# Two pairs at a time: scores and mixes merged in the first attention block, steps between engines reassigned and reordered

## The reference

```
xs = roll(x, (-3, -3));  windows of 7 x 7 -> (2048 windows, 49 tokens, 96)
q, k, v = windows @ qkv_w + qkv_b           # 12 heads of 8
attn = (q . k) / clip(|q| |k|, 1e-6) / clip(tau, 0.01) + bias + mask
out  = softmax(attn) @ v @ proj_w + proj_b  # windows and roll undone
x = x + LN(out) * g1 + b1
x = x + LN(gelu(x @ fc1_w + fc1_b) @ fc2_w + fc2_b) * g2 + b2
```

## Time and profile before

| | us |
|---|---|
| median of 3 runs (7351.54 to 7354.21) | 7353.15 |
| the profiled execution | 7355.68 |
| its span, first to last instruction | 7353.9 |
| TensorE busy (span 7353.9) | 7179.3, 98% |
| ScalarE busy | 6373.4, 87% |
| VectorE busy | 5991.6, 81% |
| GpSimd busy | 5233.9, 71% |
| 16 transfer engines, mean busy share | about 11% |

### The profile page before, as it was taken

The page is one execution under the profiler, slowest core; times in us unless marked ns, Lnnn a source line. Parts: engine busy times, 40 slices in busy tenths (PEclk is TensorE's granted clock), DMA queues, the critical chain, the costliest instruction groups (busy, mean ns, idle before and its releaser), DMA issues. The chain is left out here.

```text
span 7353.9 us, 317113 instructions
## 1 busy us (share of the span) xinstructions
PE 7179.3 (98%) x113246; PEld 5509.1 (75%) x113246; DVE 5991.6 (81%) x12718; ACT 6373.4 (87%) x12032; POOL 5233.9 (71%) x5957
## 2 busy tenths in 40 slices
PE   6999999999999999999999996999999999999999
PEld 4777777777777777777777775777777777777777
DVE  5888888888888888888888885777777777777776
ACT  5999999999999999989999986887887887887887
POOL 3777777777777777777777775666666666666665
PEclk9999999999999999999999998999999999999999
DMA  0111111111111111111111101111111111111111
GB/s 21 30 30 30 29 30 30 29 29 31 30 30 29 30 30 30 29 29 30 29 30 29 30 25 24 30 30 29 30 30 29 30 30 29 30 30 29 30 30 26
DMA packets 342624, 214.39 MB, mean 29 GB/s; under 512 B 265624, under 2 KB 341144, under 8 KB 341144
## 3 DMA queue, kind: packets, MB, share of 16 engines
q1 hardware_dynamic: 341146, 194.49, 10.7%
HBM read 78.66 MB, written 77.07 MB: 21 GB/s over the span
## 5 line engine op out<-in xcount | busy, mean ns | idle before, releaser
L881 POOL TENSOR_TENSOR swin_score<-swin_score,swin_top 113x588 f32<-113x588 f32 x1024 | 1203.1, 1175 | 743.6 <-DVE swin_top L753 743.2
L624 ACT ACTIVATE swin_probT<-swin_ps_probs 128x339 f32<-128x339 f32 x2048 | 922.1, 450 | 199.2 <-PE swin_ps_probs L481 178.2
L1553 POOL TENSOR_TENSOR plain_k_heads<-plain_k_hat,plain_head_mask 96x512 f32<-96x512 f32 x392 | 398.9, 1037 | 897.1 <-DVE plain_k_hat L1444 897.1
L481 PE MATMUL swin_ps_probs<-swin_ident,swin_prob 113*128 113x113 f32 x6144 | 991.1, 270 | 7.0 <-ACT swin_probT L624 7.0
L481 PEld LDWEIGHTS swin_ps_probs<-swin_ident,swin_prob 113*128 113x128 f32 x6144 | 667.7, 141 | 355.6 <-issue 321.5
L748 DVE TENSOR_TENSOR swin_score<-swin_ps_scores,swin_bias_tab 113x588 f32<-113x588 f32 x1024 | 777.1, 759 | 174.1 <-PE swin_ps_scores L471 172.9
L753 DVE TENSOR_REDUCE swin_top<-swin_score 113x12 f32<-113x588 f32 x1024 | 769.0, 751 | 0.2
L630 ACT ACTIVATE swin_prob<-swin_score 113x588 f32<-113x588 f32 x1024 | 719.1, 702 | 5.8 <-POOL swin_score L881 2.9
L1431 DVE TENSOR_REDUCE plain_top<-plain_ps_scores 128x6 f32<-128x384 f32 x784 | 432.7, 552 | 263.0 <-PE plain_ps_scores L1206 263.0
L784 DVE SCALAR_TENSOR_TENSOR swin_x<-swin_y,swin_y_rstd,swin_x_res 98x96 f32<-98x96 f32 x1024 | 601.1, 644 | 0.8 <-POOL swin_y_rstd L899 0.7
L495 PEld LDWEIGHTS swin_ps_mixed<-swin_probT,swin_v_heads 128*32 128x32 f32 x24576 | 422.3, 109 | 222.2 <-issue 146.0
(11 more groups left out here) (187 smaller groups left out, 20907.6 us busy)
## 6 DMA issues: line engine op xcount, KB each, us to landing
...
plain_x_in<-between_blocks SPq DMA_DIRECT2D x784, 48.0 KB, 2.2
out_dram<-plain_x SPq DMA_DIRECT2D x784, 48.0 KB, 2.0
...
```

Of the source, the lines that this page charges most:

```text
L481: last = nc.tensor.transpose(psP[:, n * QT:(n + 1) * QT], prob[0:QT, p, 2 * hp:2 * hp + 2, :].rearrange('p h k -> p (h k)'), ident[0:QT, 0 ...
L624: nc.scalar.activation(to, psP[:, 0:3 * QT], ACT.Copy).then_inc(did['probT'], 1)
L881: nc.gpsimd.tensor_tensor(view, view, bcast(top[0:QT, p % 2, :], 2, WIN), ALU.subtract).then_inc(did['shifted'], 1)
```

## The change

- `scores(d, h)` makes the scores of two pairs (2h and 2h + 1) in one step, in two column ranges of the same banks, with one semaphore step. `mix(d, h)` does the mixes of two pairs and then their sums in one step.
- `score` and `top` have four buffers, one to a pair, instead of two.
- `residual`: GpSimd multiplies y by its power in place (`scale_y`, new), and VectorE adds `x_res` in one instruction over all four pairs, in place of four instructions with multiply and add.
- `spread_values` moves from ScalarE to VectorE (two `tensor_copy`).
- The norms lie in dense banks A and B instead of B and C; `project` moves to bank A.
- The four orders are written anew. SyncE's order is unchanged.

Core of the diff (indentation cut; the last waits that only count in halves instead of pairs are left out):

```diff
-score = sb('score', [128, 2, SC])
-top = sb('top', [128, 2, heads])
+score = sb('score', [128, PAIRS, SC])
+top = sb('top', [128, PAIRS, heads])
...
+def earlier_half(g, h):
+return (g, 0) if h else (g - 1, 1)
...
-    def scores(d, p):
+    def scores(d, h):
         if exists(g + d, groups):
             pe.wait_ge(did['q_hat'], upto(g + d))
             pe.wait_ge(did['k_spread'], spread_total(g + d))
-            ug, us = before(g + d, p, 1)
-            pe.wait_ge(did['score_read'], upto(ug, us, PAIRS))
-            for half in range(2):
-                w = 2 * p + half
-                rows = HALF if half == 0 else WIN
-                for band in range(BANDS):
-                    part = slice(32 * band, 32 * band + 32)
-                    last = nc.tensor.matmul(psS[half * HALF:half * HALF + rows, band, 0:BC], q_hat[part, parity(d), w * WIN:w * WIN + rows], k_heads[part, parity(d), :, w * WIN:(w + 1) * WIN], start=True, stop=True)
+            ug, uh = earlier_half(g + d, h)
+            pe.wait_ge(did['score_read'], upto(ug, 2 * uh + 1, PAIRS))
+            for p in (2 * h, 2 * h + 1):
+                for half in range(2):
+                    w = 2 * p + half
+                    rows = HALF if half == 0 else WIN
+                    for band in range(BANDS):
+                        part = slice(32 * band, 32 * band + 32)
+                        last = nc.tensor.matmul(psS[half * HALF:half * HALF + rows, band, p % 2 * BC:(p % 2 + 1) * BC], q_hat[part, parity(d), w * WIN:w * WIN + rows], k_heads[part, parity(d), :, w * WIN:(w + 1) * WIN], start=True, stop=True)
             last.then_inc(did['scored'], 1)
...
-    def mix(d, p):
+    def mix(d, h):
         if exists(g + d, groups):
             pe.wait_ge(did['v_heads'], upto(g + d))
-            pe.wait_ge(did['probT'], upto(g + d, 2 * p + 1, 2 * PAIRS))
-            if p % 2 == 0:
-                mg, ms = before(g + d, p, 2)
-                pe.wait_ge(did['mixedT'], upto(mg, ms // 2, 2))
-            for half in range(2):
-                first = p % 2 * TT + half * WIN
-                for n in range(HB):
-                    for band in range(BANDS):
-                        last = nc.tensor.matmul(psO[32 * band:32 * band + 32, first:first + WIN], v_heads[:, (phase + d) % 4, 2 * p + half, band, n, :], probT[:, p, band * HB + n, half * HALF:half * HALF + WIN], start=n == 0, stop=n == HB - 1)
-            if p % 2 == 1:
-                for n in range(HB):
-                    for band in range(BANDS):
-                        last = nc.tensor.matmul(psO[32 * band:32 * band + 32, SUMS:SUMS + 2 * TT], sum_heads[:, n, :], all_windows(probT[:, p - 1:p + 1, band * HB + n, 0:WIN]), start=n == 0, stop=n == HB - 1)
+            pe.wait_ge(did['probT'], upto(g + d, 2 * (2 * h + 1) + 1, 2 * PAIRS))
+            mg, mh = earlier_half(g + d, h)
+            pe.wait_ge(did['mixedT'], upto(mg, mh, 2))
+            for p in (2 * h, 2 * h + 1):
+                for half in range(2):
+                    first = p % 2 * TT + half * WIN
+                    for n in range(HB):
+                        for band in range(BANDS):
+                            nc.tensor.matmul(psO[32 * band:32 * band + 32, first:first + WIN], v_heads[:, (phase + d) % 4, 2 * p + half, band, n, :], probT[:, p, band * HB + n, half * HALF:half * HALF + WIN], start=n == 0, stop=n == HB - 1)
+            for n in range(HB):
+                for band in range(BANDS):
+                    last = nc.tensor.matmul(psO[32 * band:32 * band + 32, SUMS:SUMS + 2 * TT], sum_heads[:, n, :], all_windows(probT[:, 2 * h:2 * h + 2, band * HB + n, 0:WIN]), start=n == 0, stop=n == HB - 1)
             last.then_inc(did['mixed_made'], 1)
...
-    free(('q_read', 1), ('hid', -4, 1, CHUNKS), ('x1T_low', -4), ('xT', 1))
-    turn_in(2, A)
-    free(('v_heads', 1), ('hid', -4, 2, CHUNKS), ('fc2_read', -5), ('sq_norm', 0))
-    query_norms(1, B)
-    turn_probs(-1, 1, 0)
     scores(0, 0)
     mix(-1, 0)
-    turn_probs(-1, 1, 1)
-    free(('sq_norm', 1), ('k_read', 1), ('hid', -4, 0, CHUNKS), ('proj_read', -3))
-    project(-2, C)
-    free(('xT', 2), ('q_read', 1), ('hid', -4, 1, CHUNKS), ('x1T_low', -4))
-    turn_x1(-3, A)
     turn_probs(-1, 2, 0)
-    free(('sq_norm', 1), ('v_heads', 1), ('hid', -4, 2, CHUNKS), ('fc2_read', -5))
-    output(-4, B)
+    free(('v_heads', 1), ('hid', -4, 0, CHUNKS), ('proj_read', -3), ('sq_norm', 0))
+    query_norms(1, A)
+    free(('k_read', 1), ('hid', -4, 1, CHUNKS), ('x1T_low', -4), ('sq_norm', 0))
+    key_norms(1, B)
+    free(('q_read', 1), ('hid', -4, 2, CHUNKS), ('fc2_read', -5), ('xT', 1))
+    turn_in(2, C)
     turn_probs(-1, 2, 1)
+    free(('sq_norm', 1), ('v_heads', 1), ('hid', -4, 0, CHUNKS), ('proj_read', -3))
+    project(-2, A)
+    free(('sq_norm', 1), ('k_read', 1), ('hid', -4, 1, CHUNKS), ('x1T_low', -4))
+    turn_x1(-3, B)
+    free(('xT', 2), ('q_read', 1), ('hid', -4, 2, CHUNKS), ('fc2_read', -5))
+    output(-4, C)
+    turn_probs(-1, 3, 0)
+    free(('proj_read', -2), ('sq_norm', 1), ('v_heads', 1), ('hid', -4, 0, CHUNKS))
+    hidden(-3, 0, A)
+    turn_probs(-1, 3, 1)
+    free(('x1T_low', -3), ('sq_norm', 1), ('k_read', 1), ('hid', -4, 1, CHUNKS))
+    hidden(-3, 1, B)
+    free(('fc2_read', -4), ('xT', 2), ('q_read', 1), ('hid', -4, 2, CHUNKS))
+    hidden(-3, 2, C)
+    turn_probs(0, 0, 0)
+    scores(0, 1)
     mix(-1, 1)
-    scores(0, 1)
-    turn_probs(-1, 3, 0)
-    free(('proj_read', -2), ('sq_norm', 1), ('k_read', 1), ('hid', -4, 0, CHUNKS))
-    hidden(-3, 0, C)
-    free(('x1T_low', -3), ('xT', 2), ('q_read', 1), ('hid', -4, 1, CHUNKS))
-    hidden(-3, 1, A)
-    free(('fc2_read', -4), ('sq_norm', 1), ('v_heads', 1), ('hid', -4, 2, CHUNKS))
-    hidden(-3, 2, B)
-    scores(0, 2)
-    turn_probs(-1, 3, 1)
-    free(('hid', -3, 0, CHUNKS), ('proj_read', -2), ('sq_norm', 1), ('k_read', 1))
-    keys(2, C)
-    mix(-1, 2)
-    free(('hid', -3, 1, CHUNKS), ('x1T_low', -3), ('xT', 2), ('q_read', 1))
-    queries(2, A)
-    turn_probs(0, 0, 0)
-    mix(-1, 3)
-    free(('hid', -3, 2, CHUNKS), ('fc2_read', -4), ('sq_norm', 1), ('v_heads', 1))
-    values(2, B)
-    scores(0, 3)
+    free(('hid', -3, 0, CHUNKS), ('proj_read', -2), ('sq_norm', 1), ('v_heads', 1))
+    values(2, A)
     turn_probs(0, 0, 1)
-    free(('k_read', 2), ('hid', -3, 0, CHUNKS), ('proj_read', -2), ('sq_norm', 1))
-    key_norms(2, C)
+    free(('hid', -3, 1, CHUNKS), ('x1T_low', -3), ('sq_norm', 1), ('k_read', 1))
+    keys(2, B)
+    turn_probs(0, 1, 0)
+    free(('hid', -3, 2, CHUNKS), ('fc2_read', -4), ('xT', 2), ('q_read', 1))
+    queries(2, C)
+    turn_probs(0, 1, 1)
...
-    def spread_values(d, bank):
-        if exists(g + d, groups):
-            act.wait_ge(did['v_made'], upto(g + d))
-            act.wait_ge(did['mixed_made'], upto(g + d - 4, PAIRS - 1, PAIRS))
-            for odd in range(2):
-                rows = slice(odd * HALF, odd * HALF + WIN)
-                made = psM[rows, bank, 0:WINDOWS * HP * D].rearrange('r (w n d) -> r w n d', n=HB, d=D)
-                last = nc.scalar.activation(own_heads((phase + d) % 4, odd), made, ACT.Copy)
-            last.then_inc(did['v_heads'], 1)
...
-    copy_x(2, A)
-    copy_turned(-1, 1, 0)
+    copy_turned(-1, 1, 1)
+    square_qk(1)
     exponentials(-1, 2)
-    high_x(2, A)
-    copy_turned(-1, 1, 1)
+    log_totals(-1, 0)
+    copy_turned(-1, 2, 0)
+    invert_totals(-1, 0)
+    exponentials(-1, 3)
+    copy_x(2, C)
+    high_x(2, C)
+    exponentials(0, 0)
+    copy_turned(-1, 2, 1)
+    high_x1(-3, B)
+    square_y(-2, A)
     log_norms(1)
-    high_x1(-3, A)
-    square_y(-2, C)
-    copy_turned(-1, 2, 0)
     invert_norms(1)
-    exponentials(-1, 3)
-    copy_turned(-1, 2, 1)
-    exponentials(0, 0)
-    log_totals(-1, 0)
-    invert_totals(-1, 0)
     copy_turned(-1, 3, 0)
+    exponentials(0, 1)
+    copy_turned(-1, 3, 1)
     act.preload_act_table_set(GELU_SET)
-    gelu(-3, 0, C)
-    gelu(-3, 1, A)
-    copy_turned(-1, 3, 1)
-    gelu(-3, 2, B)
+    gelu(-3, 0, A)
+    gelu(-3, 1, B)
+    gelu(-3, 2, C)
+    copy_turned(0, 0, 0)
     act.preload_act_table_set(EXP_SET)
-    exponentials(0, 1)
-    copy_turned(0, 0, 0)
-    square_qk(2)
+    copy_turned(0, 0, 1)
     log_totals(-1, 1)
-    spread_values(2, B)
-    copy_turned(0, 0, 1)
     invert_totals(-1, 1)
+    copy_turned(0, 1, 0)
...
-            dve.wait_ge(did['y_rstd'], upto(g + d))
-            dve.wait_ge(did['proj_read'], upto(g + d))
+            dve.wait_ge(did['y_norm'], upto(g + d))
             dve.wait_ge(did['x_res'], upto(g + d))
             dve.wait_ge(did['x1_turned'], upto(g + d - 1))
             dve.wait_ge(did['x1_res'], upto(g + d - 1))
-            for p in range(PAIRS):
-                last = nc.vector.scalar_tensor_tensor(x1[:, p, :], y[:, p, :], y_rstd[:, p:p + 1], x_res[:, (phase + d) % 4, p, :], ALU.mult, ALU.add)
-            last.then_inc(did['x1'], 1)
```

(69 more changed lines are left out.)

32 lines of the change are left out of this document (15 added, 17 removed).

## The result

The changed kernel takes 7700.3 us (median; 7696.5 to 7703.1), the one before, run beside it, 7352.3. The ratio is 1.047 (95%: 1.046 to 1.049): slower, as predicted, but by 348 us where 7575 stood for 222. The time is beyond the upper end of the range, 7650. The profiled execution's span is 7699.7.

A forecast was written before the change was run, and what follows sets the result against it. TensorE was taken to bound the kernel at 16.78 us a body; after the change the ring, 17.34, plus 0.33 for the load gives 17.67, +0.89 times 256, +228, forecast 7575 us, range 7420 to 7650.

The forecast's parts named there:

- The merge: On TensorE, merged steps and fewer changes of kind (14 to 7) shorten the body by 0.89 us, 16.78 to 15.89.
- (a): TensorE's projection, now in dense bank A, waits for floor_norms: 0.65 us a body, plus 0.07 of weights.
- (b): TensorE's transposes wait in three places for ScalarE's copy from the one bank of turned probabilities: 0.45 us a body.
- TensorE's own length: TensorE's body with its local waits but no wait on the chain through all engines: 17.05 us.
- the ring: Chain of waiting steps through all engines, from one projection to the next, that decides the body: 17.34 us.
- R3: Rival: floor_norms is done before the bank is needed, so the kernel is faster, 7317 down to 7125 us; chance 0.10.
- (c): Step reckoning the chain through all engines, with scale_y, the held residual and values' copies: 17.34 us a body.
- R1: Rival: VectorE's residual add isn't held up; body 17.42 us with the load, +164, 7517 us; chance 0.21.
- the case that I had priced at 0.3: GpSimd's epsilon behind gain_z also holds VectorE's residual add, making the ring some 0.3 us longer.
- (d): SyncE's later load with wrapped rows delays the keys every eighth body: 2.65 us for the ring, 0.33 a body.
- R2: Rival: the load doesn't hold the keys back; +143 or +69, 7496 to 7422 us; chance 0.15.
- R4: Rival: the add held as long as before, or values costing 1.3; ring 17.65 or more, 7655 us and up; chance 0.12.

The follow-up runs named there:

- a2_swap: Changed kernel with ScalarE's exponentials of pair 2 put ahead of its squares (square_qk); 7616.9 us.
- a3_both: Changed kernel with two edits: GpSimd's residual_x one body ahead, and ScalarE's exponentials of pair 2 ahead of its squares; 7434.7 us.
- a4_gain_late: Changed kernel with GpSimd's residual_x one body ahead and its gain_z moved behind the power of z; 7432.6 us.
- d1_one_copy: Changed kernel with residual_x one body ahead and only the first of VectorE's two values' copies made, leaving out part of the computation; 7430.8 us.
- d2: Changed kernel with residual_x one body ahead and VectorE's values' copies shortened, leaving out part of the computation; 7475.7 us.
- a1_load_early: Changed kernel with GpSimd's residual_x one body ahead, behind the power of z, so that SyncE's loads come earlier; 7567.5 us.

## Why the prediction was right in kind and wrong in size

**The merge** and **(a), (b).** TensorE's own length was predicted as 17.05. The four kernels in which the ring is shortened below it (a2_swap, a3_both, a4_gain_late, d1_one_copy) stand at 16.97 to 16.99, by three different edits. The steps are as reckoned: scores 0.82 for 0.83, mixes with sums 1.50 for 1.50, the projection 1.88 after the key norms (2030.24 to 2032.12) for 1.94, `floor_norms` 0.97, transposes 1.05 apart (2023.79 to 2024.84) where one product stands between. What the merge saves on the transposes (0.22) and on the MLP, keys and queries (0.09) was not measured by itself; it is only borne out by the sum. R3 falls on the one distance of 1.88.

**(c), the ring.** Predicted 17.34, found 17.56. From the projection to VectorE's resuming after `residual` it is 2022.37 + 17.56 - 2032.12 = 7.81, predicted 6.46 + 1.30 = 7.76. `scale_y` takes 0.82 for 0.83, `residual` holds VectorE for 1.27 where I had 1.3 (R1 falls; a4_gain_late shows what it would have been). Biases and maxima 2.71 for 2.74. The values 1.14 for 0.92 (2025.08 to 2026.22). From there to the squares 1.50 for 1.43, to the transposes 1.51 for 1.54, to the next projection 2.89 for 2.95. The term that was mis-sized is the values' copies: I had ScalarE's 0.48 each and bounds of 0.8 and 1.3, and took a value near the lower end, without a reason, for an engine of which no such copy was in the trace; VectorE takes 0.55 each. That is 0.22 of the 0.22, 56 us in 256 bodies, and d2 shows that these copies pass into the body undiminished.

How `residual` is held: the Trainium skill (SBUF — State Buffer, Who interferes with whom) says that a VectorE instruction with two SBUF inputs and a GpSimd one that reads SBUF exclude one another for a whole instruction, and that the later one waits. Here the trace agrees as to who waits. `gain_z` started first (2021.03), `residual` 0.07 later, ended 0.42 after it; GpSimd's epsilon, in its turn the later one, took 0.52, where it takes 0.20 elsewhere. `low_x` is the second case: 0.94 beside `residual_x`, 0.56 in a1_load_early, where that step lies elsewhere. My 1.3 rested on a guess ("held until shortly before the end of `gain_z`"); the rows say that the add finishes 0.42 after `gain_z`, a little sooner than its 0.56 would have it if nothing overlapped. That 1.3 came out so close is in part luck. GpSimd's epsilon behind `gain_z` did not hold the add as well, the case that I had priced at 0.3; why the instruction of 1.67 in the earlier trace rows did sit through a second step stays open.

**(d), the wrapped load.** R2 falls: the keys are late by 2.64 (predicted 2.65 for the ring), the issues of load and keys are those forecast (8.81 and 3.10). But I priced the wait as idle time alone, 0.33 a body, 85 us. 31 bodies lost 4.3 each, 134 us, and a1_load_early gives back 133. The step that failed is the last one of (d): I put nothing for what comes behind the wait. In this kernel each of these waits on TensorE is followed by some 3 us, or some 7, at half the clock; 3 us of it, in the body shown, cost 1.58 on three steps, of which the wait for the exponentials covers some 0.5. TensorE's wait for the keys over the whole span of the changed kernel (us in total, times, longest):
```profile
PE swin_ps_scores L474 <- DMA swin_k_heads<-swin_k_hat: 78.4, 28, 3.6
```
That is 2.8 each, 87 in 31 bodies, close to the 85; the other 47 came behind the waits. That they follow the clock is seen in the 31 bodies: beyond its wait a body loses 0.9 to 1.3 where the low clock lasts some 3 us, and 2.1 to 2.6 where it lasts some 7. So the miss of 125 us is 49 here, 56 in the values, and some 20 elsewhere: 10 in the second block, for which I had put nothing, and the rest in other irregular bodies and the loop's ends, for which I had taken off 6.

**The range.** R4 began at 7655, with the values at 1.3 or the add held for longer. Neither came in full, and yet the time is in R4's region by way of two smaller terms that point the same way. All my terms of unknown size had their likely error upwards (VectorE's copies, a wait with a consequence), and I had cut the range at the point where the next rival began.
